# Decoder with two layers: the last expert layer in two parts, its tiles beside the last four groups and its norms beside the second part's tiles

## The reference

```python
x1 = _layernorm(x + attn_out, g1, be1)
gate_probs = jax.nn.softmax(x1 @ Wg + bg, axis=-1)
topk_p, topk_i = jax.lax.top_k(gate_probs, K)             # K = 2 of E = 8
topk_p = topk_p / jnp.sum(topk_p, axis=-1, keepdims=True)
comb = jnp.sum(jax.nn.one_hot(topk_i, E) * topk_p[..., None], axis=-2)
h = jax.nn.gelu(jnp.einsum('bsd,edf->bsef', x1, W1) + b1, approximate=False)   # F = 512
y = jnp.einsum('bsef,efd->bsed', h, W2) + b2
moe_out = jnp.einsum('bse,bsed->bsd', comb, y)
return _layernorm(x1 + moe_out, g2, be2)                  # and then:
x = _layernorm(x + that)
```

## Time and profile before

| | us |
|---|---|
| three runs | 1670.02, 1670.45, 1673.61 |
| median | 1670.45 |
| profiled execution, its own time | 1675.12 |
| its span, first to last instruction | 1673.3 |
| PE, DVE, ACT, POOL busy in the span | 1411.3, 1126.5, 936.4, 675.2 |
| group 12 ranked | 1350.6 |
| first matmul with expert weights of a tile | 1433.7 |
| PE's last matmul | 1588.7 |

### The profile page before, as it was taken

The page is one execution under the profiler, slowest core; times in us unless marked ns, Lnnn a source line. Parts: engine busy times, 40 slices in busy tenths (PEclk is TensorE's granted clock), DMA queues, the critical chain, the costliest instruction groups (busy, mean ns, idle before and its releaser), DMA issues.

```text
span 1673.3 us, 47357 instructions
## 1 busy us (share of the span) xinstructions
PE 1411.3 (84%) x19192; PEld 1140.8 (68%) x19192; DVE 1126.5 (67%) x3503; ACT 936.4 (56%) x2474; POOL 675.2 (40%) x976
## 2 busy tenths in 40 slices
PE   6899999999979988899988899887999984799900
PEld 4788788787757776577766677765677763699800
DVE  3777777877767576787666686665785775355565
ACT  3455655655535777546875458674467852445412
POOL 5514524325142142544144442424441343245465
PEclk8799999999999999999988899998999996799955
DMA  9932212211120010100001010101000000677643
GB/s 333 385 117 74 74 58 77 71 52 46 48 89 8 9 27 15 34 27 22 11 24 31 18 34 9 27 15 30 24 28 8 15 23 25 207 225 230 183 139 95
DMA packets 112636, 124.06 MB, mean 74 GB/s; under 512 B 22049, under 2 KB 85537, under 8 KB 112161
## 3 DMA queue, kind: packets, MB, share of 16 engines
q1 hardware_dynamic: 105760, 107.26, 20.3%
q0 software_dynamic: 6656, 13.78, 2.6%
HBM read 65.72 MB, written 55.28 MB: 72 GB/s over the span
## 4 chain that ended last, share of the span: by engine, by line
PE 57%; DVE 19%; ACT 8%; issue 7%; POOL 4%; another core or an unknown queue 2%; DMA 1%; SPq 0%; DVEq 0%; POOLq 0%; ACTq 0%
PE bank L1816 5%; PE bank L1949 5%; PE bank L2196 4%; PE bank L2203 4%; PE bank L2071 3%; ACT P L1227 3%; PE bank L2036 3%; PE bank L1801 3%; PE bank L1997 3%; PE bank L1993 3%; PE bank L1986 3%; PE bank L1828 2%; PE bank L2087 2%; PE bank L1916 2%
## 5 line engine op out<-in xcount | busy, mean ns | idle before, releaser
L1816 PE MATMUL bank<-const,P 128*128 128x128 f32 x1152 | 178.1, 288 | 11.6 <-ACT P L1227 5.7
L1816 PEld LDWEIGHTS bank<-const,P 128*128 128x128 f32 x1152 | 135.9, 147 | 44.6 <-ACT P L1227 13.6
L1227 ACT ACTIVATE P<-bank,gs 128x128 f32<-128x128 f32 x512 | 142.7, 393 | 36.0 <-DVE gs L1570 35.5
L1949 PE MATMUL bank<-XT,wb 128*128 128x256 f32 x512 | 143.3, 401 | 7.6 <-ACT PT L1132 4.3
L1235 ACT ACTIVATE PT<-bank 128x512 f32<-128x512 f32 x192 | 110.9, 614 | 48.9 <-PE bank L1816 42.8
L1034 POOL TENSOR_TENSOR P<-P,gs 128x512 f32<-128x512 f32 x64 | 66.6, 1048 | 160.9 <-DVE gs L1617 160.4
L1580 DVE TENSOR_REDUCE gs<-bank 128x8 f32<-128x512 f32 x128 | 87.3, 682 | 58.4 <-PE bank L1801 32.6
L1570 DVE TENSOR_REDUCE gs<-bank 128x4 f32<-128x512 f32 x128 | 83.2, 685 | 53.4 <-PE bank L2071 50.3
L1087 POOL DMA_INDIRECT y_rows<-R,gidx x80 | 76.6, 957 | 95.6 <-DVE R L1756 81.5
L954 POOL TENSOR_SCALAR rstd<-mv 128x2 f32<-128x2 f32 x80 | 18.5, 232 | 236.9 <-DVE mv L1358 235.3
L1949 PEld LDWEIGHTS bank<-XT,wb 128*128 128x128 f32 x512 | 88.7, 193 | 24.9 <-ACT PT L1132 8.6
(11 more groups left out here) (285 smaller groups left out, 3771.6 us busy)
## 6 DMA issues: line engine op xcount, KB each, us to landing
Q<-in_wm SPq DMA_DIRECT2D x40, 578.5 KB
rows_x<-blank SPq DMA_DIRECT2D x4, 5016.0 KB, 37.6
y_mid<-PT SPq DMA_DIRECT2D x16, 512.0 KB, 3.0
y_mid<-D SPq DMA_DIRECT2D x16, 512.0 KB, 2.9
XW<-rows_x SPq DMA_DIRECT2D x40, 132.0 KB
wb<-in_wb SPq DMA_DIRECT2D x1, 4228.0 KB, 15.1
V<-in_ctxT SPq DMA_DIRECT2D x32, 128.0 KB, 2.9
P<-y_rows SPq DMA_DIRECT2D x32, 128.0 KB, 2.3
```

The source lines that it names most:

```text
L1227: ins = act.activation(P[s][:, i, 128 * g:128 * g + 128], banks[s][i][:, 128 * g:128 * g + 128], ACT.Exp, bias=gs[s][:, 0, 4 * i + g:4 * i ...
L1816: last = pe.transpose(tile(banks[s][i], t), tile(P[s][:, i, :], t), ident)
L1949: mm(half(s, 2 * (e % 2) + k), tile(B("gu"), 2 * e + k), XT[s][:, :], start=True, stop=True).then_inc(a_up_ps.of(s), 1)
```

## The change

The last expert layer is cut in two parts: part 0 holds the tokens of groups 0 to 11, part 1 those of groups 12 to 15. Each has its own rows (`rows_x0`, `rows_x1`), results (`y_rows0`, `y_rows1`), regions of 3072 and 1024 rows per expert, counts and plan. Part 0 can need 31 tiles, part 1 can need 15, so 46 tiles are worked on instead of 40. The plan of a part is made by DVE as a step `pl` behind the last ranking of the part; the count is a matmul in the same PE step `rk`.

Tiles and norms no longer have tables and waits of their own behind everything else: they are streams in the one table per engine. A tile's slot is given by `TILE_SLOTS`: slot 0 takes the first three tiles, slots 1 and 0 the next eight in turn, then slots 2, 1, 0, and from the 21st tile on all four. A slot can take a tile once its own last group is scattered. The norms use buffers of their own (`RC` in `K8`, `centred` in `V8`, output in `O`) and semaphores of their own, so that a norm can run in a slot beside a tile; loads of results for groups 0 to 11 wait for the tiles of part 0, those for groups 12 to 15 for all tiles. Each part's blanking is four DMAs, 22.7 MB in all where it was 20.5.

```diff
-CAP = 4096
-TILES = 40
+EARLY = 12
+CAP = (EARLY * NT, 4 * NT)
+TILES = (EARLY * 2 + 7, 4 * 2 + 7)
+TILE_SLOTS = (0, 0, 0) + (1, 0) * 4 + (2, 1, 0) * 3 + (3, 2, 1, 0) * 6 + (3, 2)
+XROWS = tuple(-(-(7 * c + n * NT) // 2048) * 2048 for c, n in zip(CAP, TILES))
...
+        RC = [K8[s][:, 256:512].rearrange("p (t d) -> p t d", t=T) for s in range(SLOTS)]
+        centred = [V8[s][:, 256:512].rearrange("p (t d) -> p t d", t=T) for s in range(SLOTS)]
...
             def tile(j, s):
-                yield "tx"
+                yield "m_tx"
+                i, k = number[j, s], part_of_tile(j, s)
                 if j:
                     sp.wait_ge(m_x_ps.of(s), m_x_ps.at(j - 1, s))
                     sp.wait_ge(m_row.of(s), m_row.at(j - 1, s))
+                else:
+                    sp.wait_ge(kept[s], 32 * passes)
+                    sp.wait_ge(scattered[s], 16 * 2 * T * passes)
+                sp.wait_ge(s_table, 1 + k)
+                for q in range(SLOTS):
+                    sp.wait_ge(scattered[q], 16 * 2 * T * (passes if k else EARLY // SLOTS))
...
             def finish(n, s):
+                if n == 0:
+                    yield "c_lx"
+                    sp.wait_ge(b_g_done.of(s), b_g_done.at(passes - 1, s))
+                    sp.wait_ge(kept[s], 32 * passes)
+                    load_last_x(0, s)
+                    load_last_x1(0, s)
+                if n == 0 or n * SLOTS == EARLY:
+                    yield "c_ly"
+                    if n:
+                        sp.wait_ge(c_ln_mv.of(s), c_ln_mv.at(n - 1, s))
+                    for q in range(SLOTS):
+                        sp.wait_ge(tile_y[q], 16 * T * tiles_on(q, 1 if n else 0))
+                    load_results(n, s)
...
+                if s == SLOTS - 1 and (n + 1) * SLOTS in (EARLY, groups):
+                    mm(banks[s][1][0:1, 32:32 + NE], C("full")[:, 0:1], base[:, emitted[n, s] + 1, 0, :], start=True, stop=True)
...
-            in_turn(pe, ORDERS["pe3"], [tile_of(j, s) for j in range(ROUNDS) for s in range(SLOTS)])
+            in_turn(pe, ORDERS["pe1"], [whole(n, s, first, second) for n in range(passes) for s in range(SLOTS)]
+                    + [whole(n, s, first2, second2) for n in range(passes) for s in range(SLOTS)]
+                    + [tile_of(j, s) for j, s in tiles] + [between()])
```

More of the change, by code:

```diff
@@ L871, in second2 @@
                     load_state(n + 1, s)
-            in_turn(sp, ORDERS["sp1"], [whole(n, s, first, second) for n in range(passes) for s in range(SLOTS)]
-                    + [whole(n, s, first2, second2) for n in range(passes) for s in range(SLOTS)])
-            for s in range(SLOTS):
-                sp.wait_ge(b_g_done.of(s), b_g_done.at(passes - 1, s))
-                sp.wait_ge(kept[s], 32 * passes)
-                sp.wait_ge(scattered[s], 16 * 2 * T * passes)
             def load_last_x(n, s):
@@ L927, in finish @@
                 sp.wait_ge(c_out.of(s), c_out.at(n, s))
-                sp.dma_start(token_rows(out, n, s), X1[s][:, :, :]).then_inc(written[s], 16)
-            in_turn(sp, ORDERS["sp4"], [finish(n, s) for n in range(passes) for s in range(SLOTS)])
+                sp.dma_start(token_rows(out, n, s), O[s][:, :, :]).then_inc(written[s], 16)
+            in_turn(sp, ORDERS["sp1"], [whole(n, s, first, second) for n in range(passes) for s in range(SLOTS)]
+                    + [whole(n, s, first2, second2) for n in range(passes) for s in range(SLOTS)]
+                    + [tile(j, s) for j, s in tiles] + [finish(n, s) for n in range(passes) for s in range(SLOTS)])
@@ L1106, in finish @@
                 pool.tensor_scalar(shift[s][:, :], shift[s][:, :], -1.0, None, ALU.mult).then_inc(c_ln_rstd.of(s), 1)
-            in_turn(pool, ORDERS["pool4"], [finish(n, s) for n in range(passes) for s in range(SLOTS)])
+            in_turn(pool, ORDERS["pool1"], [whole(n, s, first, second) for n in range(passes) for s in range(SLOTS)]
+                    + [whole(n, s, first2, second2) for n in range(passes) for s in range(SLOTS)]
+                    + [tile(j, s) for j, s in tiles] + [finish(n, s) for n in range(passes) for s in range(SLOTS)])
         @block.scalar
@@ L1316, in second2 @@
                 act.activation(small[s][:, 1, 0:T], small[s][:, 0, 0:T], ACT.Exp).then_inc(b_g_exp.of(s), 1)
-            in_turn(act, ORDERS["act1"], [whole(n, s, first, second) for n in range(passes) for s in range(SLOTS)]
-                    + [whole(n, s, first2, second2) for n in range(passes) for s in range(SLOTS)])
             def tile(j, s):
-                yield "tx"
+                yield "m_tx"
                 act.wait_ge(m_x_ps.of(s), m_x_ps.at(j, s))
@@ L1337, in finish @@
                 for t in range(T):
-                    last = act.activation(X1[s][:, t, :], R[s][:, t, :], ACT.Identity, bias=shift[s][:, t:t + 1], scale=rstd[s][:, t:t + 1])
+                    last = act.activation(O[s][:, t, :], RC[s][:, t, :], ACT.Identity, bias=shift[s][:, t:t + 1], scale=rstd[s][:, t:t + 1])
                 last.then_inc(c_out.of(s), 1)
-            in_turn(act, ORDERS["act4"], [finish(n, s) for n in range(passes) for s in range(SLOTS)])
+            in_turn(act, ORDERS["act1"], [whole(n, s, first, second) for n in range(passes) for s in range(SLOTS)]
+                    + [whole(n, s, first2, second2) for n in range(passes) for s in range(SLOTS)]
+                    + [tile(j, s) for j, s in tiles] + [finish(n, s) for n in range(passes) for s in range(SLOTS)])
         @block.vector
@@ L1778, in finish @@
                 for t in range(T):
-                    ins = dve.scalar_tensor_tensor(R[s][:, t, :], y[:, t, :], rstd[s][:, t:t + 1], tok(lastx[s])[:, t, :], ALU.mult, ALU.add)
+                    ins = dve.scalar_tensor_tensor(RC[s][:, t, :], y[:, t, :], rstd[s][:, t:t + 1], tok(lastx[s])[:, t, :], ALU.mult, ALU.add)
                 st2(ins)
-                norm_stats(s, st2, c_r2_mv)
-            in_turn(dve, ORDERS["dve4"], [finish(n, s) for n in range(passes) for s in range(SLOTS)])
+                norm_stats(s, st2, c_r2_mv, RC)
+            in_turn(dve, ORDERS["dve1"], [whole(n, s, first, second) for n in range(passes) for s in range(SLOTS)]
+                    + [whole(n, s, first2, second2) for n in range(passes) for s in range(SLOTS)]
+                    + [tile(j, s) for j, s in tiles] + [finish(n, s) for n in range(passes) for s in range(SLOTS)] + [between()])
         @block.tensor
@@ L2173, in second2 @@
                     .then_inc(b_k_ps.of(s), 1)
-            in_turn(pe, ORDERS["pe1"], [whole(n, s, first, second) for n in range(passes) for s in range(SLOTS)]
-                    + [whole(n, s, first2, second2) for n in range(passes) for s in range(SLOTS)] + [between()])
-            pe.wait_ge(s_count, 1)
-            for s in range(SLOTS):
-                pe.wait_ge(b_g_done.of(s), b_g_done.at(passes - 1, s))
-            mm(banks[0][0][0:1, 0:NE], C("full")[:, 0:1], base[:, groups, 0, :], start=True, stop=True).then_inc(s_count, 1)
-            pe.wait_ge(s_table, 1)
             def tile_of(j, s):
-                yield "tx"
+                yield "m_tx"
                 pe.wait_ge(tile_x[s], 16 * (j + 1))
```

221 lines of the change are left out of this document (105 added, 116 removed), and 540 rows, old and new, of tables (act1, act3, dve1, dve3).

## The result

| | before | changed |
|---|---|---|
| median of the comparison, us | 1672.14 | 1681.17 |
| ratio, with its 95% interval | | 1.0059 (1.0046 to 1.0073) |
| profiled execution's span | 1673.3 | 1678.3 |
| group 12 ranked | 1350.6 | 1362.4 |
| group 15 ranked | 1414.1 | 1475.4 |

The change made the kernel 0.6% slower; I had forecast 1.6% faster. PE's last matmul before ends at 1589.6; the 1588.7 that I gave for it ahead of the prediction, where the tables of stretches are split, is 0.9 early. The ratio is not the quotient of the two medians and differs from it by up to 0.1% here. The page's busy tenths of PE show both sides of the change: the hole at slice 34 is filled and the norms' hole at the end is shorter, but the first two slices are a tenth lower each, and there are 20 nines where there were 23.

What follows compares the result with a forecast made beforehand. PE was taken as the bound except around the last expert layer's start and after its end, where the norms' chain over POOL and DVE rules. 1350.6 + 1.5 + 109 + 74 + 56 + 56 = 1647.1 span, median 1644, range 1622 to 1670.

Steps and rivals of the forecast that it cites:

- third rival: Slower than before: group 15's chain stretched by waits between group 12's and 15's ranks, 144 not 109, time 1679; chance 0.11.
- Step 1: Ahead of group 12's rank at 1350.6: same depth of work, added plan and blanking mostly beside PE's work; 1.5 us more.
- The last sentence of my prediction: Sign of being wrong: first group-12 rank off by over 10 from 1350 would mean the new order moved earlier passes.
- Step 2: Mixed stage, group 12's rank to group 15's rank: 13.9 tiles beside groups 13 to 15, PE 89% full; 109 us.
- The 6 us for table loads: Part of the mixed stage's 109: ACT's 10 more table loads between exponentials and Gelu, bounds 0 and 12.8.
- rival of the stretched chain: Group 15's chain delayed behind tile steps waiting for weights or tables: mixed stage 144, time 1679; chance 0.11.
- Step 3: Pure tiles after group 15's rank: 19.1 tiles run as before at 3.88 each, 74 us.
- step 4: Last 13 tiles beside the first norms: POOL is the bound, 53.5 of work at 95% full, 56 us.
- second rival: Last 13 tiles held by POOL and DVE excluding each other: 17 on top of 56, time 1661; chance 0.16.
- Step 5: Norms left after PE's end: 40 of 112 POOL instructions hidden, tail 56.0 us against 84.6.

Runs made afterwards that it cites:

- e3: Changed kernel with its blanking moved from the start to 16 smaller DMAs behind the first layer's 16 stores: ratio to the kernel before 1.0051.
- e4: Kernel before with its blanking moved from the start to behind the first layer's stores: ratio to the unedited kernel before 1.0002.
- e1: Kernel before given the changed kernel's order of the groups' steps, tiles and norms keeping their old tables: 1703.6 us, ratio 1.0189.
- e2: Changed kernel with the old order of steps ahead of each engine's first tile step: 1677.2 us, ratio to the kernel before 1.0029.
- e6: Changed kernel with the tiles' Gelu replaced by Identity, so 11 table loads are gone: ratio to the kernel before 1.0119, on the second kind of chip.
- e11: Changed kernel loading the weight matrices for each slot's first tile only: ratio to the kernel before 1.0041, second kind of chip; 17.0 us less than unedited.
- e8: Changed kernel with all last-norm steps moved behind all tiles: ratio to the kernel before 1.0245, second kind of chip; 14.6 us more than unedited.
- e17: Kernel before with 48 tiles instead of 40, the eight more being empty: ratio 1.0188, 31.4 us more, 3.9 a tile.
- e14: Changed kernel with old group order, all tiles behind all groups, old tile order stretched to 46: ratio to the kernel before 1.0024, first kind of chip.
- e9: Changed kernel unedited, run again on the second kind of chip: ratio to the kernel before 1.0153.
- e12: Changed kernel with old group order, all tiles behind all groups, old tile order to tile 29: ratio to the kernel before 1.0034, second kind of chip.

## Why the prediction was wrong, step by step

Predicted span 1647.1, measured 1678.3: 31.2 more. The time of the third rival, 1679, is met by luck: its mechanism, a mixed stage of 144, did not come.

| step | predicted | measured | difference |
|---|---|---|---|
| 1. group 12's rank, from 1350.6 | +1.5 | +11.8 | +10.3 |
| 2. mixed stage | 109 | 113.0 | +4.0 |
| 3 and 4. tiles behind group 15's rank | 74 + 56 | 144.3 | +14.3 |
| 5. tail | 56.0 | 58.6 | +2.6 |

**Step 1 failed, and its mechanism was wrong.** I took "step 2077 of the order table against 2082" for the same depth of work, gave 5 either way for a new order, and priced the blanking and the plan instead. The runs showed the reverse: the blanking costs nothing that can be seen (e3, e4), the order 11 us of time and 8.7 of work left behind (e1, e2). One line is the largest part of it, PE's turning behind DVE's normalising: PE's own wait there is 12.6 where it was 0.5, and it comes and goes with the order. The last sentence of my prediction named the sign ("off by over 10 from 1350"), the sum had no room for it. How much it is worth at the end depends on what follows: 31.6 where nothing fills in, 4 in the changed kernel.

**Step 2 was right in size, partly by chance.** 113.0 for 109, and 12 table loads as read from the order. But the first tile was not near 1360: its turning is at 1375.0 and its product at 1377.9, 15.5 behind group 12's rank. The groups' work in it was 98.06 less some 13.2 tiles at 3.82, which is 47.6 and not 39; the difference is as large as the 8.7 that the order had left behind. And 13.2 tiles were done, not 13.9. The granted clock did rise (0.95 against 0.79), as assumed. The 6 us for table loads are not shown: e6 leaves anything from nothing to 12. The rival of the stretched chain (144) did not come.

**Step 3 failed in size, step 4 in its mechanism.** I had tiles at 3.88 behind the mixed stage and POOL as the bound of the last 13, at 95% full. By the count of their matmuls some 21.1 tiles ran in the 91.2 us of the first stretch, 4.3 each, and some 11.7 in the 53.1 of the second, 4.5 each. So nearly 12 of the 14.3 belong to step 3: its rate, and 0.7 tiles more than I had left for it. Step 4 was near in size, 13 x 4.5 = 59 for 56, by luck: POOL was 69% full and not the bound. What PE waits for longest is the weight load, in both stretches: 8.0 of its 15.1 idle us there, where the 40 tiles before had 2.4 idle us in all. On the other kind of chip e11 takes 17.0 away with it, and e8 measures what all the norms' steps beside the tiles cost as 8.5. The second rival, POOL and DVE held by each other, would add 17 to step 4, which lost 3, and its mechanism is rare: in the changed kernel the DVE pair of L1813 takes 0.61 to 0.63 thirteen times of sixteen, and long only where a sum of POOL lies beside it.

```profile
1609.70 1.20 DVE L1813 SCALAR_TENSOR_TENSOR K<-V,rstd,K 128x128 f32<-128x128 f32 x2
1612.30 0.61 DVE L1813 SCALAR_TENSOR_TENSOR K<-V,rstd,K 128x128 f32<-128x128 f32 x2
1653.99 1.48 DVE L1813 SCALAR_TENSOR_TENSOR K<-V,rstd,K 128x128 f32<-128x128 f32 x2 [1.09 <-issue]
```
```profile
1610.65 0.83 POOL L1122 TENSOR_TENSOR P<-P 128x256 f32<-128x256 f32 x1
1653.87 1.45 POOL L1122 TENSOR_TENSOR P<-P 128x256 f32<-128x256 f32 x2
```

Three pairs are long, by 0.59, 0.87 and 0.40, 1.9 in all. The Trainium skill (SBUF — State Buffer, Who interferes with whom) says that a DVE instruction with two SBUF inputs contends with a GpSimd instruction that reads SBUF. The trace agrees in these places and puts the price for this pair at 1.9 us, not 17; only the first of the three stands beside tiles.

**Step 5 and the six tiles were right.** The tail is 58.6 for 56.0. Its net worth is less than I had: 28.6 off the tail and 5.6 on the last tiles made 23 in my sum, and e8 measures 14.6 on the other kind. Six tiles at 3.88 are 23.3; e17 measures 23.5. Three readings in the prediction are off, by little: from PE's end to the last scatter's end it is 3.9 and not 4.8, 48.88 of 66.5 is 74% and not 70%, and the 1.5 of step 1 is in the sum but not in the clock times given on the way.

**The balance.** In the profiled executions PE's work grew by 19.8 (1411.3 to 1431.1), about what six tiles need, and its idle time fell from 262.0 to 247.2, by 14.8. I had expected it to fall by some 44 (to 217.6, the predicted 1647.1 less 1429.5 of work): the plan's gap (15.9 of it) and 25.1 of tail did go and 7.0 in the mixed stage, but 20.5 came back ahead of group 12 and 12.7 in the tiles. e2 and e14 agree on the first kind of chip (1.0029, 1.0024), so mixing hides there about what it makes. Two questions stay open: whether the old order would do as much for the mixed kernel on the second kind, and why the weights come late.

## What to carry to other kernels

When a change makes a new order of steps for engines that run in order, do not take an equal number of steps ahead of a point for equal work: compare PE's work and idle time up to that point, and look at each step that stands right behind the step of another engine that feeds it. When a wait is read from a view, see whether it is PE's own or that of its weight loads. Price the padding first (here six tiles, 3.9 each in the old place), since it is certain, while idle time that is to be filled is only partly won. And before restructuring to close a gap, read what the queue issues inside it: moving eight loads made the kernel faster by 0.25%, and the restructuring made it slower.

## What the runs showed of the hardware that I had not expected

One program takes two different times on two kinds of chip: the changed kernel has a span of 1678.3 on one and 1605.3 on the other (e9), the kernel before a median of 1672 and 1587. Group 0's rank is at 672.9 and 661.6; with the old order it is at 664.2 (e2) and 663.3 (e12), so there the kinds agree. Behind it, the stretches to group 4's, 8's and 12's rank take 19, 25 and 9 us more in the changed kernel. PE's longest waits for nothing that the profile shows ("issue") from group 0's to group 12's rank, in the changed kernel on the first chip and in e9:

```profile
PE bank L2177 <- issue: 11.2, 20, 1.3
PE bank L2123 <- issue: 4.7, 9, 1.1
PE bank L2062 <- issue: 3.9, 11, 0.5
```
```profile
PE bank L1852 <- issue: 1.7, 2, 1.2
PE bank L2177 <- issue: 1.3, 1, 1.3
```

The first three stand before runs of many matmuls of 64 columns. The granted clock is lower too: for group 0's to group 8's rank and group 8's to group 12's it is 0.95 and 0.98 on the first, 0.99 and 0.99 on the second. What makes the issue slower was not found. It matters for the verdict: the ratio of the change is 1.0153 there and 1.0059 here. A guess that no run tests is that a badly placed wait costs more where PE does not stall for itself: group 12's rank is 19.6 later than with the old order there (e9 against e12) and 11.0 here (changed against e2).
